# Attention of a gated cross-attention block on one core: x turned by VectorE and 16 small transfers instead of TensorE transposes, and the feed-forward loop written out

## The chip, the core and the metric

One core of a Trainium2 chip runs the whole program in one launch. The metric is the device time of one execution in microseconds (us); the kernel before takes 2230.28 us, the median of 3 runs. In the text PE is TensorE, DVE is VectorE, ACT is ScalarE, POOL is GpSimd and SP is the queue of SyncE that issues nearly all DMA transfers.

## What is computed

The reference, cut to what matters, is this (16 batches, 512 tokens and 512 features in x, 77 rows of context, 16 heads of 32, hidden width 2048, all float32):

```python
x = x + tanh(g_xattn) * xattn(layernorm(x), ctx)      # xattn: 16 heads, 77 keys per batch
#   q = x1 @ Wq.T + bq ; k, v from ctx ; softmax(q k^T / sqrt(32)) v ; @ Wo.T + bo
x = x + tanh(g_ffn) * ffn(layernorm(x))
#   h = x @ W1 + b1
#   h = h + (cos(theta) wr + sin(theta) wi) * (wi * sin(theta + 0.1 h)) * 0.1
#   relu(h) @ W2 + b2
```

## The kernel before, in words

Every float32 product is made of three products of parts: each operand is split into a high part (rounded by ACT, `.._0` or "hi") and a low part (the rest, by DVE, `.._1` or "lo"). `matmul3` issues the three.

Three stages follow one another. `setup` projects the context to keys and values and prepares weights. `attention` goes over the 16 batches; `ffn` goes over them again.

In `attention` each engine has a function `turn(b, parity, place)`, called once a batch, and the order in which it writes instructions is the order in which the engine runs them. A turn has four slots g = 0 to 3, one for each group of four heads. `slots_of` numbers the uses of the PSUM banks. The places are FIRST (batch 0), SECOND (batch 1), MIDDLE (2 to 14), LAST (15) and AFTER (the remainder). In a slot of a MIDDLE turn PE does, in this order:

- transposes of the probabilities of two groups back (`transpose_probs`, L907), two chunks of four transposes each;
- the scores of group g in two halves (into `pair_bank`), then in even slots a third chunk of transposes;
- the queries of the next group (`queries`, into `m_bank`; in slot 3 they are those of the next batch, from the other half of `xT`);
- the output of one tile of an earlier batch (`block_output`, `woT`, `oT`);
- in slots 1 and 2 the transposes of the next batch's x (`transpose_x`, L896), two chunks of four each;
- the product of probabilities and values (`value_product`).

`m_bank` has two banks, used in turn, so that each product into it waits for the one two before to be read out. In the value product the wait reads

```python
pe.wait_ge(m_split, n - 2)
```

and `m_split` counts what DVE has read out: `queries_lo`, `gate_output` and `heads_lo`. ACT makes in a slot the high parts of the probabilities, eight exponentials of half 0, the high part of the queries, eight exponentials of half 1, and the high part of the heads (`oT`). DVE makes the maxima (`peaks`), the reciprocal of the sums (`inverse`), the low parts, the gated output, and the layer norm: `sums` (four BATCH_NORM_STATS, L173), `statistics` (seven small instructions on 128x4) in slot 0, `normalise` (four, L198) in slot 1, both for the next batch. POOL multiplies the exponentials by the reciprocals (`probabilities`, L856), adds the output bias to the residual (`add_bias`, L867), and makes `rstd`. SP loads keys in each slot, values after the value products of slots 0 and 1, x in slot 2, and loads and stores the residual tiles.

In `ffn` the unit is a step f of 16 in a batch: 12 matmuls into `m_bank` and 12 into `pair_bank`. Batches 1 to 14 run in a loop of two batches a round (`Fori`). The stage turns x already without TensorE: four transfers write 32x32 blocks to DRAM (L1199), four read them back (L1204), and DVE transposes the blocks in place (L1360).

## Time and profile before

| | |
|---|---|
| median of 3 runs | 2230.28 us (2228.26 to 2232.8) |
| the profiled execution | 2231.27 us |
| its span, first to last instruction | 2229.5 us |
| granted TensorE clock, mean | 0.997 of full speed |
| busy share PE, DVE, ACT, POOL | 98%, 65%, 54%, 18% |
| feed-forward products | 815.10 to the end |

A share is a mean over the stages. In the tables of the timeline a row that ends in xN joins N instructions; the time given is that from the start of the first to the end of the last, and since instructions overlap by some hundredths, the distance between two starts is the better price.

### The profile page before, as it was taken

What the parts mean: (1) busy time and instruction counts of PE and PEld (TensorE: products, weight loads), DVE (VectorE), ACT (ScalarE), POOL (GpSimd) and SP (SyncE); (2) the same over time, 40 slices, a digit from 0 to 9 for tenths busy, and PEclk for the clock granted to TensorE, in tenths of its full rate; (3) what the DMA queues carried; (4) which work ended last, traced back from release to release, by engine and by line L of the source; (5) the groups of instructions that cost most, each with busy time, mean ns of one, the idle gap of its engine ahead of it and who ended that gap; (6) DMA issues with size and microseconds to landing.
All of it is one profiled execution on the core that took longest, in us unless ns stands there. A gap on an engine that the chain in (4) does not pass through costs nothing.

```text
span 2229.5 us, 30530 instructions
## 1 busy us (share of the span) xinstructions
PE 2183.2 (98%) x10385; PEld 1825.2 (82%) x10385; DVE 1438.1 (65%) x2596; ACT 1211.1 (54%) x3571; POOL 397.8 (18%) x329
## 2 busy tenths in 40 slices
PE   8989999999999989999999999999999999999999
PEld 6778888888888867888888788788888878888887
DVE  4566776676677648656656666566566566665654
ACT  3477777777777746444454444444444444544444
POOL 4033343333333311101101001011011010010110
PEclk9999999999999999999999999999999999999999
DMA  7513233333323334312223123122131231231210
GB/s 223 184 38 98 81 87 87 99 83 83 99 80 88 92 127 113 76 53 61 64 51 76 58 57 76 58 38 75 44 72 57 57 77 57 57 76 54 41 38 19
DMA packets 267311, 170.29 MB, mean 76 GB/s; under 512 B 189124, under 2 KB 203817, under 8 KB 267167
## 3 DMA queue, kind: packets, MB, share of 16 engines
q1 hardware_dynamic: 265775, 167.62, 28.2%
q8 instruction: 99, 1.62, 0.3%
q0 software_dynamic: 960, 0.64, 0.2%
q14 instruction: 45, 0.37, 0.1%
q10 hardware_dynamic: 432, 0.04, 0.0%
HBM read 108.86 MB, written 59.38 MB: 75 GB/s over the span
## 4 chain that ended last, share of the span: by engine, by line
PE 60%; DVE 1%; ACT 1%; DMA 1%; issue 0%; SPq 0%; ACTq 0%
PE m_bank L56 30%; PE pair_bank L56 30%; DVE w_split L1355 0%; DMA w_chunk<-in_L_ffn_W_dram 0%; DMA quad_scratch<-x_in 0%; DVE hidden L1388 0%; ACT relu L1315 0%; DVE turns L1384 0%; SPq L1199 0%; ACT hidden L1324 0%; ACT turns L1326 0%; DVE sine L1381 0%; DVE stats L173 0%; ACT w_split L1311 0%; DVE relu L1371 0%
## 5 line engine op out<-in xcount | busy, mean ns | idle before, releaser
L56 PE MATMUL m_bank<-xT,w_split 128*128 128x512 f32 x3072 | 740.7, 390 | 13.3 <-issue 9.4
L56 PE MATMUL pair_bank<-w_split,relu 128*128 128x512 f32 x3072 | 738.5, 389 | 3.6 <-DVE relu L1371 3.5
L56 PEld LDWEIGHTS m_bank<-xT,w_split 128*128 128x128 f32 x3072 | 577.5, 188 | 135.7 <-issue 11.5
L56 PEld LDWEIGHTS pair_bank<-w_split,relu 128*128 128x128 f32 x3072 | 576.2, 188 | 125.5 <-issue 3.8
L1331 ACT ACTIVATE sine<-turns 128x512 f32<-128x512 f32 x256 | 161.8, 632 | 386.2 <-DVE turns L1384 386.2
L1007 ACT ACTIVATE exps<-pair_bank,exp_bias 128x77 f32<-128x77 f32 x1024 | 319.5, 368 | 61.6 <-DVE exp_bias L1053 61.5
L1315 ACT ACTIVATE relu<-hidden 128x512 fp32r<-128x512 f32 x256 | 161.9, 632 | 348.3 <-PE m_bank L56 265.0
L1371 DVE SCALAR_TENSOR_TENSOR relu<-hidden,relu 128x512 fp32r<-128x512 f32 x256 | 181.2, 708 | 212.6 <-ACT relu L1315 212.6
L1388 DVE SCALAR_TENSOR_TENSOR hidden<-sine,sine_gain,hidden 128x512 f32<-128x512 f32 x256 | 197.2, 770 | 169.9 <-ACT sine L1331 169.9
L1007 ACT ACTIVATION_READ_ACCUMULATOR exps<-pair_bank,exp_bias 128x1 f32 x1024 | 255.4, 249 | 0.0
L193 POOL TENSOR_TENSOR rstd<-var_eps,minus_half 128x4 f32<-128x4 f32 x32 | 38.3, 1196 | 1202.2 <-DVE var_eps L189 1202.2
L856 POOL TENSOR_TENSOR probs<-exps,exp_inv 128x616 f32<-128x616 f32 x128 | 156.2, 1220 | 400.7 <-DVE exp_inv L1058 400.7
L1384 DVE TENSOR_TENSOR turns<-turns,sine 128x512 f32<-128x512 f32 x256 | 191.8, 749 | 8.8
L56 PE MATMUL m_bank<-xT,wqT 128*128 128x512 f32 x768 | 189.4, 395 | 0.0
L56 PE MATMUL m_bank<-woT,oT 128*128 128x512 f32 x768 | 186.0, 392 | 0.0
L1381 DVE TENSOR_SCALAR sine<-turns 128x512 f32<-128x512 f32 x256 | 122.0, 476 | 95.4 <-ACT turns L1326 94.9
L1324 ACT ACTIVATE hidden<-m_bank,columns 128x512 f32<-128x512 f32 x256 | 171.9, 672 | 4.1 <-PE m_bank L56 4.1
L1326 ACT ACTIVATE turns<-m_bank,turns_phase 128x512 f32<-128x512 f32 x256 | 173.9, 679 | 0.0
L56 PEld LDWEIGHTS m_bank<-woT,oT 128*128 128x128 f32 x768 | 144.1, 188 | 31.1
L56 PEld LDWEIGHTS m_bank<-xT,wqT 128*128 128x128 f32 x768 | 141.2, 189 | 26.8
L56 PE MATMUL m_bank<-probsT,v_diag 128*128 128x512 f32 x576 | 147.5, 401 | 3.2 <-DVE probsT L1043 3.2
L56 PE MATMUL pair_bank<-k_diag,qT 128*128 128x308 f32 x768 | 126.3, 314 | 5.1 <-PEq L276 3.0
(117 smaller groups left out, 1918.8 us busy)
## 6 DMA issues: line engine op xcount, KB each, us to landing
x_in<-in_x_dram SPq DMA_DIRECT2D x16, 1024.0 KB, 5.7
residual<-in_x_dram SPq DMA_DIRECT2D x64, 256.0 KB, 2.7
x_scratch<-residual SPq DMA_DIRECT2D x64, 256.0 KB, 2.1
x_in<-x_scratch SPq DMA_DIRECT2D x16, 1024.0 KB, 5.6
residual<-x_scratch SPq DMA_DIRECT2D x64, 256.0 KB, 3.8
out_dram<-residual SPq DMA_DIRECT2D x64, 256.0 KB, 2.1
quad_scratch<-x_in SPq DMA_DIRECT2D x60, 256.0 KB, 5.6
x_in<-quad_scratch SPq DMA_DIRECT2D x60, 256.0 KB, 4.7
```

The costliest lines, as they stand in the source:

```text
L56: mm = pe.matmul(out, stationary(s), moving(m), start=first and n == 0, stop=last and n == len(PASSES) - 1)
L193: pool.tensor_tensor(rstd[:, :], var_eps[:, :], minus_half[:, :], ALU.pow).then_inc(rstd_ready, 1)
L856: pool.tensor_tensor(probs[g // 2][:, HALF * half:HALF * (half + 1), g % 2 * GC:(g % 2 + 1) * GC] .rearrange("p n (h m) -> p n h m", m=M), ...
L1007: e = act.activation(exps[half][:, n, h * M:(h + 1) * M], pair_bank[half][:, n, h * M:(h + 1) * M], ACT.Exp, bias=exp_bias[half][:, i:i + ...
L1315: act.activation(relu[f % 2][0][:, :], hidden[f % 2][:, :], ACT.Relu).then_inc(relu_hi, 1)
L1324: act.activation(hidden[f % 2][:, :], m_bank[f % 2][:, :], ACT.Identity, bias=b1_col[:, f % FT:f % FT + 1])
L1326: act.activation(turns[:, :], m_bank[f % 2][:, :], ACT.Identity, scale=0.1 / TWO_PI, bias=turns_phase[:, f % FT:f % FT + 1]).then_inc(h_re ...
L1331: act.activation(sine[:, :], turns[:, :], ACT.Sin, scale=TWO_PI_BELOW).then_inc(sine_ready, 1)
L1371: dve.scalar_tensor_tensor(out=relu[f % 2][1][:, :], in0=hidden[f % 2][:, :], scalar=0.0, in1=relu[f % 2][0][:, :].bitcast(F32), op0=ALU.m ...
L1381: dve.tensor_scalar(sine[:, :], turns[:, :], ROUND_MAGIC, ROUND_MAGIC, ALU.add, ALU.subtract)\
L1384: dve.tensor_tensor(turns[:, :], turns[:, :], sine[:, :], ALU.subtract).then_inc(part_ready, 1)
L1388: dve.scalar_tensor_tensor(out=hidden[f % 2][:, :], in0=sine[:, :], scalar=sine_gain[:, f % FT:f % FT + 1], in1=hidden[f % 2][:, :], op0=A ...
```

## The change

There are three edits.

1. In attention the transposes of x leave PE, with their copies out of PSUM (ACT) and their low parts from PSUM (DVE). In their place DVE transposes the 32x32 blocks of `x_in` where they lie (`turn_blocks`, slot 0), SP moves the blocks into `xT` by 16 transfers inside SBUF (`move_blocks`, slot 1), ACT makes the high parts from there (`x_hi`, slot 2), and POOL and DVE make two tiles of low parts each (`x_lo`, end of slot 2).
2. Work is moved between slots: `normalise` from slot 1 to slot 0, `sums` and `statistics` from slot 0 to slot 3 of the turn before; in slot 3 of the turns SECOND and MIDDLE the output product stands ahead of the queries (`output_first`). `xT` has another layout, [tile][feature block][token], so that the query product and the first batch of the feed-forward stage read it in four strided pieces.
3. The loops of the feed-forward stage are written out.

```diff
@@ slots_of
-                    s.x = [t.next() for _ in range(2)] if g in (1, 2) and place != AFTER else None
+                    s.split_x = g == 2 and place != AFTER
+                    s.sums = g == 3 and place not in (LAST, AFTER)
...
+                    s.output_first = g == 3 and place in (SECOND, MIDDLE)
+                    if s.output_first:
+                        s.output = (b - 1, g - 2, *m.next())
@@ new, used by DVE and POOL
+            def x_lo(eng, b, parity, tiles):
+                for tile in tiles:
+                    eng.wait_ge(x_hi_ready, NT * (b - 1) + tile + 1)
+                    eng.tensor_tensor(xT[parity][1][:, tile, :], xT[parity][1][:, tile, :].bitcast(F32),
+                                      xT[parity][0][:, tile, :].bitcast(F32), ALU.subtract).then_inc(x_split, 1)
@@ SP
+                def move_blocks(b, parity):
+                    sp.wait_ge(scores_full, 2 * G * (b - 1) + 2)
+                    sp.wait_ge(blocks_turned, NT * b)
+                    for q in range(QUADS):
+                        for c in range(QUADS):
+                            sp.dma_start(xT[parity][1][c * BLOCK:(c + 1) * BLOCK, :, :].bitcast(F32)
+                                         .rearrange("p t (k a j) -> p (t k) a j", k=KT, a=QUADS)[:, :, q, :],
+                                         x_in[q * BLOCK:(q + 1) * BLOCK, :, :]
+                                         .rearrange("p t (k a j) -> p (t k) a j", k=KT, a=QUADS)[:, :, c, :])\
+                              .then_inc(blocks_moved[q], 16)
...
+                        if g == 1 and place != AFTER:
+                            move_blocks(b + 1, 1 - parity)
+                        if g == 2 and place != AFTER:
+                            for moved in blocks_moved:
+                                sp.wait_ge(moved, 16 * QUADS * (b + 1))
+                            if b + 2 >= B:
+                                load_x(x1_tiles[b + 2 - B])
+                            else:
+                                load_x(x_tiles[b + 2])
@@ TensorE
-                        if s.x:
-                            for i in range(2):
-                                transpose_x(2 * (g - 1) + i, *s.x[i], b + 1)
-                            x_split = s.x[1][0]
+                        if s.queries and s.output_first:
+                            pe.wait_ge(x_split, NT * (b + 1))
+                            queries(1 - parity, 0, *s.queries[:2])
@@ ScalarE
+                        if s.split_x:
+                            for moved in blocks_moved:
+                                act.wait_ge(moved, 16 * QUADS * (b + 1))
+                            x_hi(1 - parity, range(HALF))
@@ VectorE, attention
+                def turn_blocks(b, tiles):
+                    for tile in tiles:
+                        dve.wait_ge(normed, NT * b + tile + 1)
+                        dve.transpose(x_in[:, tile, :], x_in[:, tile, :]).then_inc(blocks_turned, 1)
@@ feed-forward stage
-                batch(0, 0, False)
-                with eng.Fori(1, B - 2, 2) as b:
-                    batch(b, 1, False)
-                    batch(b + 1, 0, False)
-                batch(B - 1, 1, True)
+                for b in range(B):
+                    batch(b, b % 2, b == B - 1)
```

The order on DVE around the end of slot 3 (`qT_1` is the low part of the queries, `residual` the gated output, `oT_1` the low part of the heads). Before, from the reciprocal of half 0 on:

```order
L1058 RECIPROCAL exp_inv<-exp_sum 128x8
L1062 SCALAR_TENSOR_TENSOR qT_1<-m_bank,columns,qT_0 128x512
L1074 SCALAR_TENSOR_TENSOR residual<-m_bank,tanh_g,residual 128x512
L1058 RECIPROCAL exp_inv<-exp_sum 128x8
L1068 TENSOR_TENSOR oT_1<-m_bank,oT_0 128x512
L1043 TENSOR_TENSOR probsT<-t_bank,probsT 128x512 x2
```

After, from the gated output on:

```order
L1113 SCALAR_TENSOR_TENSOR residual<-m_bank,tanh_g,residual 128x512
L1101 SCALAR_TENSOR_TENSOR qT_1<-m_bank,columns,qT_0 128x512
L180 BN_STATS stats<-x_in 128x6 x2
L1097 RECIPROCAL exp_inv<-exp_sum 128x8
L186 TENSOR_TENSOR moments<-stats 128x4
L187 TENSOR_TENSOR moments<-stats 128x4
L188 TENSOR_TENSOR moments<-stats 128x4
L190 TENSOR_SCALAR mean<-moments 128x4
L191 SCALAR_TENSOR_TENSOR moments<-moments 128x4
L193 TENSOR_SCALAR moments<-moments 128x4
L196 TENSOR_TENSOR var_eps<-moments 128x4
L1107 TENSOR_TENSOR oT_1<-m_bank,oT_0 128x512
```

The statistics now stand between the last reciprocal and the low part of the heads, and the output is read out ahead of the queries.

The order on DVE in slot 0, after its maxima. Before:

```order
L1043 TENSOR_TENSOR probsT<-t_bank,probsT 128x512
L173 BN_STATS stats<-x_in 128x6 x2
L1058 RECIPROCAL exp_inv<-exp_sum 128x8
L1062 SCALAR_TENSOR_TENSOR qT_1<-m_bank,columns,qT_0 128x512
L173 BN_STATS stats<-x_in 128x6 x2
```

After:

```order
L1077 TENSOR_TENSOR probsT<-t_bank,probsT 128x512
L205 TENSOR_SCALAR x_in<-x_in,mean,rstd 128x512 x4
L1097 RECIPROCAL exp_inv<-exp_sum 128x8
L1093 STREAM_TRANSPOSE x_in<-x_in 128x512 x2
L1101 SCALAR_TENSOR_TENSOR qT_1<-m_bank,columns,qT_0 128x512
L1113 SCALAR_TENSOR_TENSOR residual<-m_bank,tanh_g,residual 128x512
```

Ahead of the low part of the queries there are now four normalising instructions and two block transposes, where two BN_STATS were.

The order on ACT at the end of slot 2 and the start of slot 3, after (before, the x copies were from PSUM, two in slot 1 and two in slot 2, all ahead of `oT_0`):

```order
L1038 ACTIVATE exps,exp_sum<-pair_bank,exp_bias 128x77 x8
L1029 ACTIVATE xT_0<-xT_1 128x512 x2
L1066 ACTIVATE oT_0<-m_bank 128x512
L1029 ACTIVATE xT_0<-xT_1 128x512 x2
L1025 ACTIVATE probsT<-t_bank 128x512 x2
```

All four copies of x now stand in slot 2, two of them behind the heads.

## Rows read from the trace of the kernel before

**Rows 1.** Window in attention: PE, PEld, DVE, ACT, POOL busy, clock, DMA share, GB/s

```profile
420.00:480.00 60.00, 60.00 (x335) 52.25 (x334) 41.54 (x87) 43.55 (x203) 20.36 (x17) 1.00 0.35 94
```

**Rows 2.** Timeline, PE, slot 3 and slot 0 (start, length, instructions)

```profile
431.42 1.03 PE L907 MATMUL t_bank<-ident,probs 128*128 128x128 f32 x8
432.21 1.94 PE L56 MATMUL pair_bank<-k_diag,qT 128*128 128x308 f32 x12
433.99 2.88 PE L56 MATMUL m_bank<-xT,wqT 128*128 128x512 f32 x12
436.71 2.92 PE L56 MATMUL m_bank<-woT,oT 128*128 128x512 f32 x12
439.46 2.24 PE L56 MATMUL m_bank<-probsT,v_diag 128*128 128x512 f32 x9
...
450.06 2.24 PE L56 MATMUL m_bank<-probsT,v_diag 128*128 128x512 f32 x9
```

**Rows 3.** Groups by line: transposes (busy, mean ns | idle before, releaser)

```profile
L907 PE MATMUL t_bank<-ident,probs 128*128 128x128 f32 x640 | 86.5, 274 | 5.1 <-DVE xT L1043 4.4 <-DVE probsT L1043 0.8
L896 PE MATMUL t_bank<-ident,x_in 128*128 128x128 f32 x256 | 33.5, 274 | 3.6 <-DVE x_in L198 3.6
L1360 DVE STREAM_TRANSPOSE x_in<-x_in 128x512 f32<-128x512 f32 x60 | 38.9, 687 | 0.0
```

**Rows 4.** Timeline, ACT, end of slot 3

```profile
437.51 0.72 ACT L1014 ACTIVATE qT<-m_bank,columns 128x512 fp32r<-128x512 f32 x1
438.08 0.37 ACT L1007 ACTIVATE exps<-pair_bank,exp_bias 128x77 f32<-128x77 f32 x1
```

**Rows 5.** Timeline, DVE, end of slot 3, slot 0 and slot 1

```profile
440.72 0.20 DVE L1058 RECIPROCAL exp_inv<-exp_sum 128x8 f32<-128x8 f32 x1 [0.30 <-ACT exps L1007]
442.37 0.69 DVE L1068 TENSOR_TENSOR oT<-m_bank,oT 128x512 fp32r<-128x512 f32 x1 [1.45 <-ACT oT L1034]
442.98 1.28 DVE L1043 TENSOR_TENSOR probsT<-t_bank,probsT 128x512 fp32r<-128x512 f32 x2
444.18 0.79 DVE L1050 TENSOR_REDUCE peak<-pair_bank 128x8 f32<-128x616 f32 x1
...
445.99 0.68 DVE L1043 TENSOR_TENSOR probsT<-t_bank,probsT 128x512 fp32r<-128x512 f32 x1
...
450.40 0.17 DVE L179 TENSOR_TENSOR moments<-stats 128x4 f32<-128x4 f32 x1
...
451.18 0.75 DVE L1074 SCALAR_TENSOR_TENSOR residual<-m_bank,tanh_g,residual 128x512 f32<-128x512 f32 x1
...
456.58 1.91 DVE L198 TENSOR_SCALAR x_in<-x_in,mean,rstd 128x512 f32<-128x512 f32 x4
```

**Rows 6.** Timeline, POOL, end of slot 3

```profile
441.00 1.22 POOL L856 TENSOR_TENSOR probs<-exps,exp_inv 128x616 f32<-128x616 f32 x1 [1.81 <-DVE exp_inv L1058]
```

**Rows 7.** Timeline, POOL and DVE side by side in turn SECOND

```profile
152.03 1.29 POOL L867 TENSOR_TENSOR residual<-residual,bo_rows 128x512 f32<-128x512 f32 x1
152.51 0.83 DVE L1053 TENSOR_SCALAR exp_bias<-peak 128x8 f32<-128x8 f32 x1
```

**Rows 8.** Timeline, DVE in feed-forward beside POOL's residual additions

```profile
2149.49 1.49 DVE L1381 TENSOR_SCALAR sine<-turns 128x512 f32<-128x512 f32 x1
```

**Rows 9.** What one L1384 takes (min/median/max ns)

```profile
L1384 DVE TENSOR_TENSOR turns<-turns,sine x256: 691/693/1666, 821.5 to 2219.4; 128x512 f32<-128x512 f32 x128
```

**Rows 10.** Timeline, SP queue, one batch of the feed-forward stage

```profile
1111.60 5.75 SPq L1199 DMA_DIRECT2D quad_scratch<-x_in  x4
1120.89 1.76 SPq L1204 DMA_DIRECT2D x_in<-quad_scratch  x4
```

**Rows 11.** Timeline and waits, PE in the feed-forward stage

```profile
1087.91 1.75 PE L56 MATMUL m_bank<-xT,w_split 128*128 128x512 f32 x7
1091.03 1.32 PE L56 MATMUL m_bank<-xT,w_split 128*128 128x512 f32 x5 [1.37 <-issue]
...
PE m_bank L56 <- issue: 9.4, 6, 1.7
```

More of the change, by code:

```diff
@@ L160, in gated_attention_ffn_kernel, with by_tiles, tiles_of @@
         xT = [[sb(whole, f"xT{s}_{i}", [P, KT, N], F32R) for i in range(2)] for s in range(2)]
+        def by_tiles(part, kt):
+            return part[:, :, kt * P:(kt + 1) * P]
+        def tiles_of(row):
+            return row.rearrange("p (t n) -> p t n", t=NT)
         x_loaded = sem(whole, "x_loaded")
@@ L704, in attention @@
             bo_rows = sb(st, "bo_rows", [P, D])
+            blocks_turned = sem(st, "blocks_turned_a")
+            blocks_moved = [sem(st, f"blocks_moved{q}") for q in range(QUADS)]
+            x_hi_ready = sem(st, "x_hi_ready")
+            x_split = sem(st, "x_split")
             t_full = sem(st, "t_full_a")
@@ L768, in slots_of @@
                         queries_done = s.queries[0]
-                    if g >= 2 and place != FIRST:
+                    if g >= 2 and place != FIRST and not s.output_first:
                         s.output = (b - 1, g - 2, *m.next())
@@ L871, in turn @@
                     for g, s in enumerate(slots_of(b, place)):
+                        if g == 0 and place != AFTER:
+                            rstd_of(pool, b + 2)
                         if place != FIRST:
@@ L875, in turn @@
                             probabilities(2 * G * b + 2 * g + 1, g, 0)
-                        if g == 0 and place != AFTER:
-                            rstd_of(pool, b + 2)
                         if s.score:
                             probabilities(2 * G * b + 2 * g + 2, g, 1)
+                        if s.split_x:
+                            x_lo(pool, b + 1, 1 - parity, range(HALF))
                 for i in range(G // 2):
@@ L889, in _ @@
             def _(pe):
-                def transpose_x(kt, n, bank, b):
-                    if kt == 0:
-                        pe.wait_ge(normed, NT * (b + 1))
-                    if not (isinstance(n, int) and n <= 2):
-                        pe.wait_ge(t_split, n - 2)
-                    for tile in range(NT):
-                        tr = pe.transpose(t_bank[bank][:, tile * P:(tile + 1) * P],
-                                          x_in[:, tile, kt * P:(kt + 1) * P], ident[:, :])
-                    tr.then_inc(t_full, 1)
                 def transpose_probs(b, g, c, n, bank):
@@ L969, in turn @@
                             last_heads = s.values[0]
-                        if s.queries:
+                        if s.queries and not s.output_first:
                             if g == 3:
-                                pe.wait_ge(t_split, x_split)
+                                pe.wait_ge(x_split, NT * (b + 1))
                             queries(parity ^ (g == 3), (g + 1) % G, *s.queries[:2])
@@ L999, in bank_hi, with x_hi @@
                     act.activation(dst, t_bank[bank][:, :], ACT.Copy).then_inc(t_hi, 1)
+                def x_hi(parity, tiles):
+                    for tile in tiles:
+                        act.activation(xT[parity][0][:, tile, :], xT[parity][1][:, tile, :].bitcast(F32),
+                                       ACT.Copy).then_inc(x_hi_ready, 1)
                 def exponentials(unit, half):
@@ L1027, in turn @@
                             exponentials(2 * G * b + 2 * g + 2, 1)
[L1028 to L1030 removed]
+                        if s.split_x:
+                            for moved in blocks_moved:
+                                act.wait_ge(moved, 16 * QUADS * (b + 1))
+                            x_hi(1 - parity, range(HALF))
                         if s.finish:
@@ L1035, in turn @@
                                .then_inc(m_hi, 1)
+                        if s.split_x:
+                            x_hi(1 - parity, range(HALF, NT))
                 over_batches(act, turn)
@@ L1054, in peaks @@
                        .then_inc(bias_ready, 1)
+                def turn_blocks(b, tiles):
+                    for tile in tiles:
+                        dve.wait_ge(normed, NT * b + tile + 1)
+                        dve.transpose(x_in[:, tile, :], x_in[:, tile, :]).then_inc(blocks_turned, 1)
                 def inverse(unit, half):
@@ L1229, in _ @@
                 outputs(0, False)
-                with sp.Fori(1, B - 2) as b:
+                for b in range(1, B - 2):
                     regroup_x(b + 1)
```

63 lines of the change are left out of this document (33 added, 30 removed).

## The prediction

> **What bounds the kernel now.** I read the stretches first. In attention PE is busy for all 60 of 60 us at the full clock, DVE for 41.5 and ACT for 43.6 [rows 1]. So PE is the bound there, and an instruction taken off it is worth its distance on PE's timeline, as long as the other engines still answer in time. Then PE's timeline over one slot 3 and one slot 0: the products follow each other without a gap [rows 2]. Eight transposes take 0.79 us (431.42 to 432.21), the scores 1.78, the queries 2.72, the output 2.75. Last DVE's timeline over the same stretch, to see how much later its answers may come: it waits 0.30 and 1.45 us [rows 5], so its reserve is small. In the feed-forward stage I looked for PE's gaps. Six are put down to "issue", 9.4 us together [rows 11]: the loop of seven rounds returns six times.
>
> **What goes.** (a) Sixteen transposes of x a batch. Those of x (L896) have the mean of those of the probabilities (L907), 274 ns [rows 3], so a batch saves 2 x 0.79 = 1.58 us of PE. The 14 turns MIDDLE and LAST, where PE has no gap, save 14 x 1.58 = 22.1 us. (b) In the first two turns PE waited for x: 3.6 us on L198 and 4.4 us on the low parts, 8.0 together [rows 3]. The new way starts with four BN_STATS and the statistics ahead of the first maxima (about 3 us of DVE), so I take half, 4 us, between bounds of 8 and 0. (c) The loop's six jumps. At one, 7 matmuls and the gap take 3.12 us (1087.91 to 1091.03), where 7 x 0.227 = 1.59 would do; 0.227 is 2.72 over 12. That is 1.53 lost where the gap reads 1.37 [rows 2, 11]. Scaled, 9.4 becomes 10.5 us. I expect all of it back: the written-out attention code runs at more matmuls in 60 us with no gap [rows 1].
>
> **What comes, off the path.** ACT's four copies of x stay four. SP gets 16 transfers of 64 KB, in pieces of 128 bytes, 8192 in all. The nearest rows are the feed-forward stage's four stores, also 8192 pieces of 128 bytes: 9.3 us from the first issue to the loads that wait for the last (1111.60 to 1120.89) [rows 10]. The blocks are turned at the end of slot 0. SP first issues six value loads, at 1.76 / 4 = 0.44 us each as the loads of [rows 10] 2.6 us, and a last transfer may need 2 us to land, so the move ends some 14 us after slot 1 begins. A slot is 0.79 + 1.78 + 2.72 + 2.75 and a value product of 2.1, 10.1 us [rows 2]; ACT ends its exponentials of half 1 about 9 us into slot 2 and only then asks for the blocks, at 19. 5 us are left: hidden. x's low parts are then ready near 3 to 4 us of slot 3, and PE asks at 5.3.
>
> **What comes, on the path.** It is the order around the end of slot 3. I count from the first transpose of slot 3 (431.42 is 0).
>
> - Slot 2, end. DVE's two low parts of x use two SBUF operands while POOL makes its own two. Rows show what that does: an exp_bias of 128x8 took 0.83 us beside a POOL addition [rows 7], a TENSOR_SCALAR in feed-forward took 1.49 [rows 8], and L1384, with both inputs in SBUF, takes 691 at least and 1666 ns at most [rows 9]. DVE waits until POOL's instruction ends. Two low parts, 1.2, and a wait of some 1.2 make DVE 2.4 us later in slot 3. The exponentials of half 0, which ended at 6.1 (437.51 less 431.42) [rows 4], end at 8.5.
> - Output now comes ahead of queries: the queries end at 0.79 + 1.78 + 2.75 + 2.72 = 8.04, instead of 5.29. In ACT's queue the queries' high part stands ahead of the exponentials of half 1, so these start at 8.5 + 0.57 = 9.1 (437.51 to 438.08) [rows 4], instead of 6.66.
> - The reciprocal of half 1 comes 2.64 later (438.08 to 440.72) [rows 4, 5]: 11.7.
> - Now the statistics, 0.78 (450.40 to 451.18) [rows 5]. But the reciprocal sets off POOL's multiplication 0.28 later, and that lasts 1.22 [rows 6]. The small TENSOR_SCALARs in the statistics are of the kind that waited in [rows 7], so about 1.1 us more: 11.9 + 0.78 + 1.1 = 13.8.
> - Then, without a wait between: low part of the heads 0.61, two low parts of probabilities 1.20, maxima 1.81 (444.18 to 445.99), a third low part 0.6, normalising 1.9, reciprocal 0.1, two block transposes 1.2 (687 ns each, overlapping as the others do) [rows 3, 5]: 7.4, which makes 21.2. The queries' low part, 0.75, ends at 22.0.
> - The value product of slot 0 uses the bank that this low part reads, and waits for it. Before, it started at 450.06, that is 18.64 [rows 2]. It loses 3.4 us. The smaller stalls on the way (the value product of slot 3 behind the gated output, the third chunk of transposes) are inside this figure. Slots 1 and 2 bring DVE back in time, since normalising has left slot 1.
>
> There are 14 such ends of slot 3 (SECOND and MIDDLE): 14 x 3.4 = 47.6 us.
>
> **The page's rule.** The rows above show that DVE's small scalar instruction waits beside POOL. The Trainium skill (SBUF — State Buffer, Who interferes with whom) says that the pair of ports that VectorE and GpSimd share is an exclusive lock for a whole instruction, taken by tensor_scalar in its fast modes and by two-input instructions with both inputs in SBUF. By this rule the statistics and the low parts of x do wait, as forecast; if it did not hold here, the sum would be that of rival 2. The skill (DMA: Bandwidth & Descriptors, Rules for kernel authors) also speaks against 16 transfers on 32 partitions each: under 64 KB a transfer is mostly overhead, and transfers to disjoint partitions serialize. No row of this trace shows such transfers.
>
> **Sum.** 47.6 - 22.1 - 4 - 10.5 = +11.0 us on the profiled execution's 2231.27: 2242.3. The median is 1.0 lower than that execution, so 2241.
>
> **The rivals.**
>
> 1. *POOL gets in between DVE's two low parts of x.* In [rows 8] DVE's next instruction stood queued and still let one of POOL's pass. Here it would be the bias addition, if its residual tile has come; SP loads it behind the 16 transfers, which speaks against. It moves everything by 1.2 us: 14 x 1.2 = 17 more, 2258.
> 2. *No waits for POOL.* If the statistics slip past the multiplication and the low parts of x don't meet, the end is at 8.8 + 2.64 + 0.2 + 0.78 + 7.4 + 0.75 = 20.6, a stall of 2.0: 28 - 22.1 - 4 - 10.5 = -8.6, 2222. For it: the multiplication starts 0.28 after the reciprocal, so a part of the statistics does slip past.
> 3. *The other side: ScalarE and VectorE take up the whole delay.* It decides at a stall under 1.6 + 14.5/14 = 2.6 us a boundary; with none, 2231.3 - 22.1 - 4 - 10.5 = 2195, less 1 is 2194. Against it: the chain above has no gap left in it.
> 4. *The move is late.* If each of the 16 transfers took as long to issue as one of the four stores, 5.75 / 4 = 1.44 us, the move would take 23 us, and with what stands ahead 9 more than ACT leaves; at 8 us a batch, 2350. Against it: a quarter of the pieces each. It decides where the move takes 14 us or more.
>
> **How the numbers follow.** Under 0.2% (4.5 us) a change of this kernel cannot be told from none. Forecast, 2234 to 2250: 0.40. Rival 1, 2250 to 2266: 0.18. Rival 2, 2214 to 2226: 0.18. Rival 3 proper, below 2214: 0.08. Rival 4, above 2266: 0.07. In between, 2226 to 2234: 0.09. So faster 0.26, same 0.10, slower 0.64. The range that leaves out 2 in 10 is 2214 to 2262; that of the forecast alone is 2234 to 2250.
>
> **What the changed profile would show.** Right: no L896 rows; MIDDLE turns 3.4 - 1.58 = 1.8 us longer on PE's timeline; PE idle before the value product of slot 0, released by DVE's low part of the queries; mean and moments instructions of 0.6 us or more instead of 0.17; low parts of x on DVE above 1 us; no idle put down to issue in feed-forward. Wrong, if turns are 1.6 us shorter (rival 3), if statistics keep 0.17 (rival 2), or if ACT waits for the moved blocks (rival 4).

## The result

| kernel | median | against the kernel before (95% interval) |
|---|---|---|
| before | 2228.3 us (2226.2 to 2232.8, 5 runs) | |
| after | 2240.9 us (2239.1 to 2241.7, 5 runs) | 1.0053 (1.0039 to 1.0067) |

The change makes the kernel 0.5% slower, as forecast (2241). The 2230.28 us ahead of the prediction is the median of the first three of the five runs of before. All runs are of the fast state. The ratio is worked out from all runs and need not be the quotient of the two medians.

The experiments were run in three groups: 1 to 4, then 6, 7, 8 and 10, then 5, 9, 11 and 12, each with its own runs of the kernel before (medians 2228.8, 2230.1 and 2231.1 us), and each ratio is to those. A difference in us between kernels of different groups, such as "less than after", is therefore good to some 3 us; where it matters the difference of the ratios stands beside it.

The profiled execution of after has a span of 2239.1 us, that of before 2229.5: 9.6 us to find. Three lines of after's page (span, busy time, DMA packets):

```profile
span 2239.1 us, 29108 instructions
PE 2164.8 (97%) x10129; PEld 1797.5 (80%) x10129; DVE 1484.2 (66%) x2628; ACT 1212.7 (54%) x3571; POOL 446.3 (20%) x361
DMA packets 402481, 186.93 MB, mean 83 GB/s; under 512 B 324293, under 2 KB 338986, under 8 KB 402336
```

PE has 256 instructions less and is busy for 18.4 us less (2183.2 before), yet the span is longer: PE now waits. Its waits between 165 and 780 us, the turns SECOND to LAST of attention (engine and product that waited, whom for: total, times, longest). In before the same stretch has no such row.

```profile
PE m_bank L56 <- DVE residual L1113: 21.4, 14, 2.2
PE m_bank L56 <- DVE qT L1101: 8.5, 14, 0.6
PE t_bank L934 <- DVE probsT L1077: 3.5, 10, 0.4
```

Each of the 14 ends of slot 3 has its set of waits. One of them, on PE's timeline (start, length, instructions, in brackets the idle time before and who ended it); it answers to [rows 2]:

```profile
393.93 1.03 PE L934 MATMUL t_bank<-ident,probs 128*128 128x128 f32 x8
394.72 1.95 PE L56 MATMUL pair_bank<-k_diag,qT 128*128 128x308 f32 x12
396.50 2.93 PE L56 MATMUL m_bank<-woT,oT 128*128 128x512 f32 x12
399.27 2.89 PE L56 MATMUL m_bank<-xT,wqT 128*128 128x512 f32 x12
403.46 2.31 PE L56 MATMUL m_bank<-probsT,v_diag 128*128 128x512 f32 x9 [1.30 <-DVE residual L1113]
405.62 1.03 PE L934 MATMUL t_bank<-ident,probs 128*128 128x128 f32 x8
...
408.73 0.63 PE L934 MATMUL t_bank<-ident,probs 128*128 128x128 f32 x4 [0.38 <-DVE probsT L1077]
...
415.47 2.32 PE L56 MATMUL m_bank<-probsT,v_diag 128*128 128x512 f32 x9 [0.64 <-DVE qT L1101]
417.63 1.03 PE L934 MATMUL t_bank<-ident,probs 128*128 128x128 f32 x8
```

Slot 3 and slot 0 take 23.70 us here (393.93 to 417.63). The same two took 20.71 in before, where no slot 3 or slot 0 waits. So a boundary loses 2.99 us, while the three idle times shown add up to 2.32: each wait costs some 0.2 us more than it shows. The rows say where it is: without a wait two products overlap (2.93 long, the next start 2.77 later), behind a wait they don't, and a value product behind a wait takes 2.31 us instead of 2.24. Over all 14 boundaries, the starts of slots on PE's timeline give 44.3 us (eleven between 2.98 and 3.05; the others 3.17, 3.49 and 4.61).

DVE's timeline over the same end of slot 3 answers to [rows 5]:

```profile
395.37 2.38 DVE L812 TENSOR_TENSOR xT<-xT,xT 128x512 fp32r<-128x512 f32 x2
...
402.49 0.20 DVE L1097 RECIPROCAL exp_inv<-exp_sum 128x8 f32<-128x8 f32 x1 [0.53 <-ACT exps L1038]
402.61 0.71 DVE L1113 SCALAR_TENSOR_TENSOR residual<-m_bank,tanh_g,residual 128x512 f32<-128x512 f32 x1
...
405.52 0.20 DVE L1097 RECIPROCAL exp_inv<-exp_sum 128x8 f32<-128x8 f32 x1 [0.35 <-ACT exps L1038]
...
405.94 1.10 DVE L190 TENSOR_SCALAR mean<-moments 128x4 f32<-128x4 f32 x1
...
407.30 0.68 DVE L1107 TENSOR_TENSOR oT<-m_bank,oT 128x512 fp32r<-128x512 f32 x1
...
413.44 1.25 DVE L1093 STREAM_TRANSPOSE x_in<-x_in 128x512 f32<-128x512 f32 x2
414.62 0.71 DVE L1101 SCALAR_TENSOR_TENSOR qT<-m_bank,columns,qT 128x512 fp32r<-128x512 f32 x1
```

ACT's first exponential of half 1 and POOL's multiplication behind the second reciprocal:

```profile
402.88 0.37 ACT L1038 ACTIVATE exps<-pair_bank,exp_bias 128x77 f32<-128x77 f32 x1
```

```profile
405.80 1.22 POOL L891 TENSOR_TENSOR probs<-exps,exp_inv 128x616 f32<-128x616 f32 x1 [1.81 <-DVE exp_inv L1097]
```

Behind the reciprocal of half 1 DVE does not stand still until the low part of the queries. The instruction for the mean takes 1.10 us, where its fastest is 170 ns; it ends at 407.04, and POOL's multiplication ran from 405.80 to 407.02. The two low parts of x take 2.38 us where two of that shape take 1.29 undisturbed (shown below).

**The whole account**, from the starts of slots and stages on the two timelines, after less before. The boundaries: +44.3. Slots 1 and 2 without the transposes of x: 10.12 + 10.59 instead of 11.03 + 11.47 in most turns; over the 14 turns -24.9. The start up to the first slot 3 of SECOND: 170.00 instead of 172.18, -2.2. From the last slot 3 to the feed-forward stage's first product: 40.43 instead of 38.03, +2.4; PE waits there 1.13 us for the gated output (at 804.19) and 0.45 us for probabilities (at 807.68), which it does not in before. The feed-forward stage, from its first product to the end: 1398.03 instead of 1407.99, -10.0, with no idle time put down to issue left. Sum +9.6, the whole of the 9.6.

### The profile page after: what moved, and what is told of

The parts are those of the page before. It is cut to its first block, busy times and chain, and to the rows that moved or that the text cites. A ratio compares the mean times of both kernels' runs of the same rounds, so it can differ in the third digit from the quotient of the medians.

```text
span 2239.1 us, 29108 instructions
## 1 busy us (share of the span) xinstructions
PE 2164.8 (97%) x10129; PEld 1797.5 (80%) x10129; DVE 1484.2 (66%) x2628; ACT 1212.7 (54%) x3571; POOL 446.3 (20%) x361
## 3 DMA queue, kind: packets, MB, share of 16 engines
q8 instruction: 79, 1.29, 0.2%
## 4 chain that ended last, share of the span: by engine, by line
PE 60%; DVE 2%; ACT 1%; DMA 0%; issue 0%; ACTq 0%
PE m_bank L56 30%; PE pair_bank L56 30%; DVE w_split L1402 1%; DVE hidden L1435 0%; DMA w_chunk<-in_L_ffn_W_dram 0%; DVE turns L1431 0%; ACT relu L1362 0%; ACT hidden L1371 0%; DVE sine L1428 0%; ACT turns L1373 0%; DVE relu L1418 0%; DVE stats L180 0%; ACT w_split L1358 0%; DVE x_in L205 0%; ACT sine L1378 0%
## 5 line engine op out<-in xcount | busy, mean ns | idle before, releaser
L56 PEld LDWEIGHTS m_bank<-probsT,v_diag 128*128 128x128 f32 x576 | 107.1, 190 | 67.7 <-issue 41.0
```

Of the source, the lines that this page charges most:

```text
L56: mm = pe.matmul(out, stationary(s), moving(m), start=first and n == 0, stop=last and n == len(PASSES) - 1)
```

## Experiments

Theory: the 3 us of a boundary are one delay. Two ways of equal length lead to ACT's exponentials of half 1 (DVE's low parts of x held up beside POOL; output ahead of queries, through ACT's queue), and from there DVE's chain, with a wait for POOL inside the statistics, leads to the low part of the queries in slot 0. Rivals: the waits are separate losses; the order of output and queries is the whole cost; the 16 transfers are.

### 1. The loop alone

```diff
-                batch(0, 0, False)
-                with eng.Fori(1, B - 2, 2) as b:
-                    batch(b, 1, False)
-                    batch(b + 1, 0, False)
-                batch(B - 1, 1, True)
+                for b in range(B):
+                    batch(b, b % 2, b == B - 1)
...
-                with sp.Fori(1, B - 2) as b:
+                for b in range(1, B - 2):
```

The second part is SP's own loop over the batches.

> The kernel before with one part of the change alone: the feed-forward loop of seven rounds is written out, attention stays as it was. My theory (each return of TensorE's loop loses about 1.7 us, of which its waits show 1.6 as issue): 10 us less than before, about 2218, and no idle time put down to issue on PE. Rival (other engines are as late as the jump, so the gap only changes its name): under 2 us less, 2226 to 2228.

2218.7 us, ratio 0.9954 (0.9941 to 0.9966): 10.1 less than the 2228.8 of before beside it. Its waits of PE from 810 us on hold no issue; they are the whole answer:

```profile
PE m_bank L56 <- DVE w_split L1352: 3.9, 1, 3.9
PE pair_bank L56 <- DVE relu L1368: 3.2, 4, 1.0
```

So what the change does to attention alone costs 12.6 + 10.1, near 23 us (19.6 in the account of the two profiled executions), and the loop hides 10 of them. Why a return costs this much is not shown here, only that it goes with the loop.

### 2. Statistics ahead of the reciprocal

```diff
+                        if s.sums:
+                            statistics(dve, b + 3)
                         if s.score:
                             inverse(unit + 2, 1)
-                        if s.sums:
-                            statistics(dve, b + 3)
```

> The changed kernel, with the statistics moved ahead of the reciprocal of half 1, into the 0.35 us in which DVE waits for the exponentials. There they cannot meet POOL's multiplication. My theory (what ends last at a boundary is DVE's chain from the exponentials of half 1 on, and the mean instruction of 1.10 us instead of 0.17 is in it): the chain is 0.9 us shorter, each boundary 0.8 to 1.0 us, in all 11 to 14 us less: 2227 to 2230, and the mean instruction takes 0.17 us. Rival (PE loses its time to the wait of slot 3's value product, which this does not touch): only the two waits in slot 0 shrink and the next turn gives it back, 2238 to 2241.

2238.0 us, ratio 1.0042 (1.0028 to 1.0056): 2.9 less, not 11 to 14. The mean instruction takes 0.17 us as expected, but the time is that of the rival (2238 to 2241). DVE's timeline of this kernel:

```profile
402.58 0.17 DVE L190 TENSOR_SCALAR mean<-moments 128x4 f32<-128x4 f32 x1
...
403.47 0.69 DVE L1107 TENSOR_TENSOR oT<-m_bank,oT 128x512 fp32r<-128x512 f32 x1 [0.27 <-ACT oT L1066]
...
406.10 0.67 DVE L1087 TENSOR_SCALAR exp_bias<-peak 128x8 f32<-128x8 f32 x1
```

Two things ate most of the 0.9 us; the low part of the queries in slot 0 starts 20.34 us after the first transpose of slot 3 instead of 20.69. DVE, now early, waits 0.27 for the heads, whose value product had itself started late (the wait of slot 3). And POOL, which no longer has to wait for the variance, makes its bias addition at 405.45 to 406.75, just beside the next `exp_bias`: 0.67 instead of 0.17. A boundary still costs 2.6 to 3.0 (one 4.25). A wait removed from one place on DVE came back at another small instruction 2 us on.

### 3. The gated output earlier

```diff
+                        if s.output_first:
+                            gate_output(*s.output)
                         if s.score:
                             inverse(unit + 1, 0)
-                        if s.output_first:
-                            gate_output(*s.output)
```

> The changed kernel, with the gated output of slot 3 moved ahead of the reciprocal of half 0 on DVE, so that slot 3's value product can start 0.5 to 0.65 us earlier (POOL's bias addition then ends last). My theory (the waits of a boundary share one delay, which DVE's chain sets at the value product of slot 0): PE comes earlier to slot 0 and waits longer there, the sum of a boundary stays at 3.0 us, total within 3 us of 2241. Rival (each wait is a loss of its own): 14 x 0.6 = 8 us less, 2232.

2240.9 us, ratio 1.0053 (1.0037 to 1.0070). PE's timeline over one boundary of this kernel:

```profile
404.92 2.31 PE L56 MATMUL m_bank<-probsT,v_diag 128*128 128x512 f32 x9 [0.59 <-DVE residual L1113]
...
410.91 0.63 PE L934 MATMUL t_bank<-ident,probs 128*128 128x128 f32 x4 [1.11 <-DVE probsT L1077]
...
417.65 2.31 PE L56 MATMUL m_bank<-probsT,v_diag 128*128 128x512 f32 x9 [0.60 <-DVE qT L1101]
```

The first wait shrinks from 1.30 to 0.59 and the second grows from 0.38 to 1.11. Two thirds of all idle time at a boundary stood in after's table against the gated output, and this takes half of it away for nothing: 12 of the 14 boundaries still cost 2.98 to 3.34 us, the other two 3.41 and 3.89. Waits of one boundary share one delay; the rival (2232) falls.

### 4. Queries first

```diff
-                    s.output_first = g == 3 and place in (SECOND, MIDDLE)
+                    s.output_first = False
```

The count by which the queries of a turn find their number (`queries_done`) is moved to match.

> The changed kernel, with the queries of slot 3 ahead of the output again, as before the change. PE then has to wait for the low parts of x, which end 3.8 us after slot 3 begins, 1.2 us after PE comes (2.6), but the high part of the queries and so the exponentials of half 1 are no longer 2 us later. My theory (the exponentials of half 1 start the chain that ends last; but they can then only start after those of half 0, 0.5 us earlier than now): the wait of slot 3's value product goes, that for x costs 1.2 to 1.4, slot 0's shrink by 0.5; 0 to 10 us less, 2231 to 2241. Rival (the order of output and queries is the whole cost of a boundary): 20 us or more less, under 2221. The other rival (x comes too late for this order): slower than 2241.

2242.1 us, ratio 1.0062 (1.0049 to 1.0075), 1 us above the range of my theory and far from the 2221 of the first rival. It is also on the side of the other rival (slower than 2241): PE does wait for x here. Most boundaries cost 3.05 to 3.18. DVE's two low parts of x end at 397.65 and PE's queries start at 397.71, after 1.12 us of idle time; the exponentials of half 1 then wait for those of half 0 instead of for the queries. The reciprocal of half 1 comes at 405.49, where after has 405.52, though the two boundaries start within 0.1 us of each other.

### 5. All low parts of x on POOL

```diff
-                            x_lo(pool, b + 1, 1 - parity, range(HALF))
+                            x_lo(pool, b + 1, 1 - parity, range(NT))
...
-                        if s.split_x:
-                            x_lo(dve, b + 1, 1 - parity, range(HALF, NT))
```

> The changed kernel with all four low parts of x on POOL, none on DVE, so that DVE's 2.4 us (two instructions and the wait for POOL's) at the end of slot 2 are gone. My theory (they and the order of output and queries set the exponentials of half 1 side by side, not one after the other: ACT has the high part of the queries ahead of them, at 8.4 us of slot 3 in any case): the exponentials of half 0 start 1 to 2 us earlier, those of half 1 do not, the wait of slot 3's value product shrinks and those of slot 0 grow, total 2236 to 2242. Rival (the two add up): 14 x 1.5 to 2 us less, 2212 to 2220. Other rival (PE waits for POOL's fourth low part, which ends about when PE comes): over 2245.

2241.2 us, ratio 1.0050 (1.0037 to 1.0063). This takes the other way out, and nothing is won either: a boundary costs 2.93 to 3.2. PE waits 0.56, 0.97 and 0.63 us at the three places. The first `exp_bias` takes 0.94 us beside POOL's four low parts, and ACT now waits 0.49 us for the queries before the exponentials of half 1. Experiments 4 and 5 together show the two ways of equal length: removing either one alone gives nothing. In after the exponentials of half 0 end at 8.4 us of slot 3 and the queries at 8.2.

### 6. First block transposes behind the gated output

```diff
-                        if g == 0 and place != AFTER:
-                            turn_blocks(b + 1, range(HALF))
                         if s.output_first:
                             gate_output(*s.output)
...
                         if s.output and not s.output_first:
                             gate_output(*s.output)
+                        if g == 0 and place != AFTER:
+                            turn_blocks(b + 1, range(HALF))
```

> The changed kernel, with the first two block transposes of slot 0 moved behind the low part of the queries and the gated output. My theory (DVE's chain sets the end of a boundary at the low part of the queries of slot 0, for which the value product waits 0.64 us): that low part comes 1.2 us earlier, the wait goes, and with it about 0.2 us that a wait costs beyond what it shows: 14 x 0.85 = 12 us less, 2229. The wait of 1.30 us in slot 3 and that of 0.38 stay. Rival (the same delay comes out at the next product instead, since the transposes are only moved by two instructions): within 3 us of 2241.

2232.0 us, ratio 1.0003 (0.9993 to 1.0013): 8.9 less than after (11 by the ratios). The value product of slot 0 starts without a wait and 11 of the 14 boundaries cost 2.14 to 2.30, 0.85 less, as forecast. Three cost 3.3 to 4.2 in the profiled execution, two of them with a value product of 3.9 us (see the last section), and slots 1 and 2 now take 0.16 us a turn more (20.87 instead of 20.71), 2.3 us in all, which the forecast did not have. This one move of an instruction pair brings the kernel back to the time of before. The low part of the queries was the end of the chain.

### 7. Four straight transfers instead of 16

```diff
-                    for q in range(QUADS):
-                        for c in range(QUADS):
+                    for t in range(QUADS):
+                        sp.dma_start(xT[parity][1][:, t, :].bitcast(F32), x_in[:, t, :]).then_inc(blocks_moved[t], 16)
...
-                                sp.wait_ge(moved, 16 * QUADS * (b + 1))
+                                sp.wait_ge(moved, 16 * (b + 1))
```

ACT's wait changes in the same way. This kernel leaves out the exchange of blocks between partitions, so it computes something else.

> The changed kernel, with four straight transfers of 128 partitions and 2 KB a partition in place of the 16, so that the blocks of x stay where they are and the values of attention are other ones. My theory (the 16 transfers are hidden; all that they do on the path is to make POOL's bias additions late, which the value product of slot 3 feels by less than 0.7 us): 2236 to 2241, ACT's copies start at the same time as before. Rival (the number and the shape of the transfers cost, by DMA traffic beside keys, values and residuals): 2230 or less.

2237.4 us, ratio 1.0029 (1.0020 to 1.0038). 3.5 less than after (5 by the ratios), inside my theory's range. A boundary costs 2.99 as before, but there are none above 3.14, where after has 3.49 and 4.61. SP's queue in this kernel, and below it in after (16 of a quarter of the size):

```profile
375.56 2.48 SPq L829 DMA_DIRECT2D xT<-x_in  x4
```

```profile
420.32 10.75 SPq L830 DMA_DIRECT2D xT<-x_in  x16
431.11 1.85 SPq L837 DMA_DIRECT2D residual<-in_x_dram  x1
```

A transfer costs SP 0.62 us of 256 KB in pieces of 2 KB and 0.67 us of 64 KB in pieces of 128 bytes. Four times the bytes do not make the issue longer, but the number of transfers is not the whole price either: the stores of [rows 10], 256 KB in pieces of 128 bytes, took 1.44 us each. What decides between them is not shown.

### 8. Residual tiles ahead of the 16 transfers

```diff
+                        early = g in (1, 2) and place not in (FIRST, SECOND, AFTER)
+                        if early:
+                            reload_residual(b - 1, g + 1)
                         if g == 1 and place != AFTER:
                             move_blocks(b + 1, 1 - parity)
...
-                        if g < 3 and place not in (FIRST, SECOND):
+                        if g < 3 and place not in (FIRST, SECOND) and not early:
                             reload_residual(b - 1, g + 1)
```

> The changed kernel, with SP's loads of the residual tiles in slots 1 and 2 ahead of the 16 transfers and of the wait for them. POOL then doesn't wait 7 and 3.7 us for them. My theory: POOL was not on the path, but for the gated output of slot 3 by at most 0.1 us, so 2238 to 2242; if POOL's low parts of x come earlier the lock on DVE's two shrinks and it is up to 10 us less. Rival (the late residual tiles are what the value product of slot 3 waits for): the wait of 1.30 us goes, 14 x 1.5 = 21 less, 2220.

2240.9 us, ratio 1.0040 (1.0026 to 1.0054), no different from after (the two intervals overlap). POOL had waited 7.09 us in slot 2 for a residual tile behind the transfers; that wait was free. The value product of slot 3 still waits 1.31 us with the addition long done, so the rival (2220) falls.

### 9. The 16 transfers ten microseconds later

```diff
-                        if g == 1 and place != AFTER:
-                            move_blocks(b + 1, 1 - parity)
...
                             load_values(sp, b, g, values_loaded[g])
+                        if g == 1 and place != AFTER:
+                            move_blocks(b + 1, 1 - parity)
```

> The changed kernel, with SP's 16 transfers of x moved behind the load of the values in slot 1, which is about 10 us later; nothing else changes. It measures how near the hidden move is to the path. My theory (the move takes about 11 us to issue and 2.3 to land, ends 3 us before ACT asks for it, so here 6 to 7 us after; ACT's high parts of x and, behind them, the heads and probabilities wait that long): PE loses 6 to 7 us a batch more, 15 x 6.5 = 98, in all 2330 to 2345, and ACT waits for the moved blocks. Rival (the 3 us of waits at a boundary take up a part of it): 2280 to 2300. Rival (only x itself waits, no queue behind it): under 2270.

2340.7 us, ratio 1.0489 (1.0475 to 1.0502), inside my theory's range, though in part for another reason. SP's, ACT's and PE's timeline of one boundary:

```profile
416.85 10.76 SPq L830 DMA_DIRECT2D xT<-x_in  x16
```

```profile
429.40 1.15 ACT L1029 ACTIVATE xT<-xT 128x512 fp32r<-128x512 f32 x2 [6.25 <-DMA xT<-x_in]
```

```profile
433.81 5.49 PE L56 MATMUL m_bank<-xT,wqT 128*128 128x512 f32 x12 [3.86 <-DVE xT L812]
440.44 2.31 PE L56 MATMUL m_bank<-probsT,v_diag 128*128 128x512 f32 x9 [1.15 <-DVE residual L1113]
```

ACT waits until 429.40; issues end at 427.61 and land about 2 us later. A boundary costs 7.4 to 11.9 instead of 3.0. PE is idle for 3.86 us, and then the queries take 5.49 us instead of 2.89: the granted clock between 424 and 443 us is 0.82, so that a part of it ran at the lower level of 1.2 GHz. Over the 14 boundaries PE loses 6.6 us more each than in after, as forecast, but only some 4 us of that are idle time; most of the rest are products at the lower clock, which the theory did not have, so the number is partly luck. The move as it stands in after costs at most what experiment 7 shows, but its reserve is small: there it ends 15.7 us after slot 1 begins (13.4 and 2.3 to land), and ACT asks at 19.2.

### 10. All orders moved

On top of 2, 6 and 8: DVE's low parts of x between the two maxima of slot 3; in slot 3 ACT's exponentials of half 1 ahead of the high part of the queries, and DVE's low part of the queries behind the reciprocal.

```diff
                             peaks(unit + 1, 0)
+                            if g == 3:
+                                x_lo(dve, b + 1, 1 - parity, range(HALF, NT))
                             peaks(unit + 2, 1)
...
                         if s.score:
                             exponentials(2 * G * b + 2 * g + 2, 1)
+                        if s.queries and s.output_first:
+                            queries_hi(0, *s.queries[:2])
...
+                        if s.output_first:
+                            queries_lo(0, *s.queries[1:])
```

> The changed kernel with the orders that the theory of DVE's and ACT's chain asks for, all at once. DVE: its two low parts of x go from the end of slot 2 to slot 3, between the maxima of half 0 and of half 1; statistics ahead of the reciprocal of half 1; low part of the queries behind that reciprocal; first block transposes behind the gated output. ACT: in slot 3 the exponentials of half 1 ahead of the high part of the queries. SP: residual tiles ahead of the 16 transfers. My theory: the exponentials of half 0 start 2.4 us and those of half 1 3 us earlier, PE has no wait of over 0.2 us left at a boundary, and 14 x 3.0 = 42 us go: 2199, with a range of 2195 to 2208. Rival (the locks between POOL and DVE and the waits only move to other instructions): 2215 or more.

2211.3 us, ratio 0.9909 (0.9894 to 0.9924): 30 less than after, 12 short of my number and 3 outside its range, on this side of the rival (2215 or more). A boundary costs 0.75 instead of 3.0 in 11 of 14 cases. Short of the 42 us are those 0.75 (11.4 in all), 0.16 us a turn in slots 1 and 2 as in experiment 6 (2.2), and the start: the first slot 3 of SECOND begins at 174.15 instead of 170.00. PE's one wait left, and DVE's line that it waits for:

```profile
391.63 3.04 PE L56 MATMUL m_bank<-xT,wqT 128*128 128x512 f32 x12 [0.30 <-DVE xT L812]
```

```profile
388.18 1.29 DVE L1082 TENSOR_TENSOR probsT<-t_bank,probsT 128x512 fp32r<-128x512 f32 x2 [0.83 <-ACT probsT L1028]
...
390.21 0.17 DVE L1092 TENSOR_SCALAR exp_bias<-peak 128x8 f32<-128x8 f32 x1
390.29 1.29 DVE L812 TENSOR_TENSOR xT<-xT,xT 128x512 fp32r<-128x512 f32 x2
```

DVE's low parts of x take 1.29 here, since POOL's two are over. But DVE had waited 0.83 us for the probabilities, which stood in ACT's queue behind the last two copies of x.

### 11. The same with ACT's order as in after

```diff
-                        if s.queries and not s.output_first:
+                        if s.queries:
                             queries_hi((g + 1) % G, *s.queries[:2])
                         if s.score:
                             exponentials(2 * G * b + 2 * g + 2, 1)
-                        if s.queries and s.output_first:
-                            queries_hi(0, *s.queries[:2])
```

DVE's low part of the queries goes back with it.

> The kernel with all orders moved, but with ACT's order in slot 3 as the change made it: exponentials of half 1 behind the high part of the queries, and DVE's low part of the queries ahead of the second sums. My theory: the exponentials of half 1 start 1.6 us later and DVE's chain at the end of slot 3 about 0.9 us, but with the statistics and the block transposes out of that chain there are some 0.5 us to spare: 2211 to 2219. Rival (output ahead of queries, through ACT's queue, is the main cost of the change): 2225 or more.

2222.0 us, ratio 0.9961 (0.9949 to 0.9973): 10.7 above the last one, 3 above my range. A boundary costs 1.74. Of ACT's order, then, one microsecond a boundary, once the other way to the exponentials is out: PE waits 0.42 us for the low parts of x (0.30 in experiment 10), 0.37 us for POOL's probabilities of half 1, and 0.23 us for the low part of the queries, behind an `exp_bias` that took 0.94 us beside a bias addition again.

### 12. The best version

```diff
                                 bank_hi(probsT[0][:, c, :], *s.probs[c])
+                        if g == 3:
+                            x_hi(1 - parity, range(HALF, NT))
...
-                        if s.split_x:
-                            x_hi(1 - parity, range(HALF, NT))
```

> The kernel with all orders moved, and in ACT's queue the last two high parts of x behind the two high parts of the probabilities of slot 3 instead of ahead of them. In its profile a boundary still lost 0.75 us: PE waited 0.30 us for DVE's low parts of x, which came late because DVE had itself waited 0.83 us for ACT's probabilities, held up by those copies. My theory: DVE starts slot 3 0.8 us earlier, the wait goes, 14 x 0.5 to 0.7 us less, 2202 to 2205. Rival (ACT's copies come just as late for the low parts of x as the probabilities did): 2209 to 2213.

2205.0 us, ratio 0.9881 (0.9867 to 0.9896), the fastest: 26 us below the 2231.1 of before beside it. Its waits of PE from 165 to 770 us:

```profile
PE m_bank L56 <- DVE residual L1118: 3.8, 5, 1.5
PE m_bank L56 <- DVE xT L812: 0.9, 3, 0.5
```

Four of the 14 boundaries cost 0.27 us, the others 0.31 to 1.85, and what they wait for now comes from DMA. One that lost 0.92, DVE's and POOL's timeline; then DVE at one that lost 1.56:

```profile
385.96 2.39 DVE L812 TENSOR_TENSOR xT<-xT,xT 128x512 fp32r<-128x512 f32 x2
```

```profile
385.96 1.84 POOL L905 TENSOR_TENSOR residual<-residual,bo_rows 128x512 f32<-128x512 f32 x1 [0.74 <-DMA residual<-in_x_dram]
```

```profile
474.29 1.29 DVE L180 BATCH_NORM_STATS2 stats<-x_in 128x6 f32<-128x512 f32 x2 [1.20 <-DMA x_in<-in_x_dram]
```

In the first a residual tile lands late and puts POOL's addition beside DVE's low parts of x; in the second x of a later batch lands late. SP loads both behind the 16 transfers. That these are the rest is read from the timeline alone and was not tried.

## Why the prediction was right

**What bounds the kernel.** Right. PE had no reserve in attention, and the orders of the others decided.

**The chain.** It held link by link. From the first transpose of slot 3 (393.93): exponentials of half 0 end 8.4 (forecast 8.5), queries end 8.2 (8.0), exponentials of half 1 start 8.95 (9.1), reciprocal 11.6 (11.7), heads' low part 13.4 (13.8), low part of the queries starts 20.7 (21.2), value product 21.5 (22.0). The boundary costs 2.99 instead of 3.4, because the statistics with their wait took 1.78 us instead of 2.1, and the links up to the reciprocal and those behind the statistics 0.1 less each. Experiments 3, 4, 5 and 6 show that this chain and not the sum of single waits sets the time; 2 shows that one of its links can't be taken out alone.

**The signs.** Not all came as I had named them. Of the statistics only the mean instruction grew (1.10 us); the moments kept 0.12 to 0.16, since three stood ahead of POOL's multiplication and the rest behind it. The MIDDLE turns are 1.2 us longer, not 1.8. And I looked for PE's idle time before the value product of slot 0: it is there (0.64 us), but the largest wait of a boundary (1.30 us) stands before that of slot 3, for the gated output, which the prediction had called a smaller stall. The sum was right, its place on PE's timeline only in part.

**The terms**, forecast and measured: boundaries 47.6 and 44.3; transposes 22.1 and 24.9; start 4 and 2.2; loop 10.5 and 10.0 (10.1 by itself in experiment 1). The transposes were mis-sized: I took 0.79 us for eight, the distance to the next start, and the two slots became 0.91 and 0.88 shorter. The value product behind the transposes of x was longer too: 2.17 us to the next start, where it takes 2.07 without them (450.06 to 452.13). On PE's timeline of before:

```profile
460.20 1.03 PE L896 MATMUL t_bank<-ident,x_in 128*128 128x128 f32 x8
460.99 2.33 PE L56 MATMUL m_bank<-probsT,v_diag 128*128 128x512 f32 x9
463.16 1.03 PE L907 MATMUL t_bank<-ident,probs 128*128 128x128 f32 x8
```

The way from the last slot 3 to the feed-forward stage, +2.4, I had no term for. The misses nearly cancel (+11.0 and +9.6). The forecast also stood on a median of before of 2230.3, which over five runs is 2228.3, so the rise of the medians is 12.6 where the sum said 10.7. That 2240.9 stands beside 2241 is in part luck.

**The move.** Hidden, as forecast; it ends at 15.7 us where I said 14, and 3.5 us are left where I said 5. Experiment 9 shows what lies behind this reserve.

**The page's rule.** The Trainium skill (SBUF — State Buffer, Who interferes with whom) has VectorE and GpSimd lock each other out of the pair of ports that they share for a whole instruction. The traces agree: the mean instruction took 1.10 us beside POOL and ended 0.02 after POOL's, and took 0.17 when moved away from it. The other rule (DMA: Bandwidth & Descriptors, Rules for kernel authors), that transfers to disjoint partition halves serialize, did not decide: the 16 were issued 0.67 us apart and landed in 2.1 to 4.2 us, the median in 2.3, and the move stayed hidden. Whether they serialized is not shown.

**The rivals.** Rival 1 did not come: the residual tile was late, as said against it, and POOL's bias addition came after. Rival 2: the low parts took 2.38 and the mean 1.10, so POOL was waited for, though three instructions of the statistics did slip past, as said for it. Rival 3 fell with 44.3 us in waits. Rival 4 is experiment 9, and its price of 8 us a batch for 9 us of delay is near the 6.6 measured there, where ACT waits 6.25 us at the boundary shown, but that has the lower clock in it; its condition was not met.

## What to carry over

Where several waits of one period add up to a constant, look for the chain that they share before mending one: here half of the wait that looked largest was taken away for nothing, and moving one pair of block transposes, which no wait named, was worth 9 us or more. Two ways of equal length have to be shortened together. When work is moved off the busiest engine, put what replaces it where the next engine has idle time, and away from an instruction on which that engine answers; the change cost 12.6 us as it was made, and with the orders around it moved it gains 26, of which 10 are the loop's.

## What I had not expected of the hardware

- A long wait of PE can cost a second time. After 2.19 us of idle time at one boundary of after, the value product took 3.89 us instead of 2.31; the granted clock of that stretch of 5 us is 0.66 (a mean over both of its levels, 2.4 GHz, which is 1.00, and 1.2), in a kernel whose mean is 0.995. In after, waits of up to 1.80 us at a boundary were followed by value products of 2.30 to 2.32. The length of the wait alone does not tell: experiment 8 has one of 1.85 us followed by 3.88, and experiment 6 two of 2.33 and 2.36 followed by 3.89 and 3.88 and one of 2.45 followed by 2.32. What decides is open. The windows (stretch, length, PE, PE's loads, DVE, ACT and POOL busy, granted clock, DMA share, GB/s):

```profile
343.00:353.00 10.00, 10.00 (x54) 8.58 (x53) 6.08 (x10) 7.25 (x28) 6.67 (x5) 1.00 0.65 194
353.00:358.00 5.00, 3.13 (x14) 2.25 (x12) 4.40 (x8) 3.25 (x19) 1.66 (x2) 1.00 0.32 106
358.00:363.00 5.00, 4.67 (x18) 3.84 (x19) 3.94 (x13) 3.10 (x18) 2.74 (x3) 0.66 0.37 111
```

And the two value products that speak against the length alone, experiment 8 and then experiment 6:

```profile
714.67 3.88 PE L56 MATMUL m_bank<-probsT,v_diag 128*128 128x512 f32 x9 [1.85 <-DVE residual L1116]
```

```profile
754.16 2.32 PE L56 MATMUL m_bank<-probsT,v_diag 128*128 128x512 f32 x9 [2.45 <-DVE residual L1113]
```

- The lock of DVE and POOL follows small instructions about. An `exp_bias` of 128x8 took 0.17 us undisturbed, and 0.67 (experiment 2), 0.94 (11) or 1.06 (after, at 353.66) when a bias addition of 1.3 us on POOL had begun just before; each ended within 0.03 us of POOL's end.
- A short wait costs PE some 0.2 us more than its idle time shows: 2.32 shown and 2.99 lost over three waits.
